# A gated feed-forward stage moved into the attention's block, with its last products in another order

## The reference, cut to what matters

```
x = layernorm(x + attention(x))                  # third norm
gate = silu(x @ dequant(gate_wq, gate_scale).T)  # 512 -> 1376
up   = x @ dequant(up_wq, up_scale).T            # 512 -> 1376
x = layernorm(x + (gate * up) @ dequant(down_wq, down_scale).T)   # 1376 -> 512, last norm
```

## Time and profile before

| | |
|---|---|
| time, median of 3 runs | 2475.66 us (2474.8 to 2475.94) |
| the profiled execution, its own time | 2476.66 us |
| its span, first to last instruction | 2474.6 us |
| PE busy | 2373.2 us, 96% of the span |
| DVE, ACT, POOL busy | 72%, 64%, 51% |
| mean granted clock of PE | 0.984 of full |
| the gated stage, first gate product to the end | 2338.26 us to 2474.6 us |

### The profile page before, as it was taken

One profiled execution on the slowest core, in us unless ns is written; L12 is line 12 of the kernel. 1 busy time (PEld: TensorE's weight loads), 2 busy tenths in 40 slices (PEclk: granted clock), 3 DMA queues, 4 the chain that ended last, 5 costly groups with the idle time before them and its releaser, 6 DMA issues. The chain is left out here.

```text
span 2474.6 us, 48904 instructions
## 1 busy us (share of the span) xinstructions
PE 2373.2 (96%) x15424; PEld 1359.8 (55%) x15624; DVE 1791.4 (72%) x3234; ACT 1591.7 (64%) x3327; POOL 1255.2 (51%) x1002
## 2 busy tenths in 40 slices
PE   6999999999999999999999998789999999999897
PEld 3555555555555555555555555445555555555443
DVE  5677787787777777787777776577777777778522
ACT  7676776776776776776776775365556555656422
POOL 4465555555556556556556569443434343454223
PEclk8999999999999999999999999989999999999899
DMA  7343343343343343343343441320110110100000
GB/s 249 101 132 108 115 130 107 115 131 108 113 133 105 115 133 106 114 134 105 113 134 105 131 146 50 138 89 1 43 44 1 44 44 1 43 18 1 1 0 34
DMA packets 113827, 218.79 MB, mean 88 GB/s; under 512 B 9632, under 2 KB 43040, under 8 KB 111360
## 3 DMA queue, kind: packets, MB, share of 16 engines
q1 hardware_dynamic: 113536, 215.28, 27.0%
HBM read 212.10 MB, written 3.15 MB: 87 GB/s over the span
## 5 line engine op out<-in xcount | busy, mean ns | idle before, releaser
L989 ACT ACTIVATE E<-wq,cst 128x128 f32<-128x128 f32 x1024 | 311.7, 389 | 3.0 <-PEq L298 3.0
L256 DVE SCALAR_TENSOR_TENSOR xc<-bank,taps,xc 128x511 f32<-128x511 f32 (+2 forms) x384 | 284.9, 742 | 35.5 <-ACT xc L243 18.0
L1919 POOL TENSOR_TENSOR qT<-qT,qrot 128x512 f32<-128x512 f32 x64 | 81.2, 1269 | 370.1 <-DVE qrot L1809 370.1
L1282 POOL TENSOR_TENSOR acc<-acc,sq 128x512 f32<-128x512 f32 x112 | 173.1, 1545 | 183.3 <-ACT sq L1001 183.3
L1273 POOL TENSOR_TENSOR xw<-xt,wdec 128x384 f32<-128x384 f32 x128 | 106.4, 831 | 294.1 <-DVE xt L1124 150.7
L1166 DVE SCALAR_TENSOR_TENSOR u<-xc,D,bank 128x512 f32<-128x512 f32 x128 | 95.6, 747 | 205.8 <-PE bank L814 194.2
L1105 DVE TENSOR_TENSOR E<-E,cbm 128x1024 f32<-128x1024 f32 x128 | 242.8, 1897 | 0.8
L59 PE MATMUL bank<-xhi,wx 128*128 128x512 f16 x640 | 242.8, 379 | 0.0
L60 PE MATMUL bank<-xlo,wx 128*128 128x512 f16 x640 | 242.8, 379 | 0.0
L61 PE MATMUL bank<-xhi,wx 128*128 128x512 f16 x640 | 242.6, 379 | 0.0
L1268 POOL TENSOR_TENSOR ecs<-ecs,xcC 128x768 f32<-128x768 f32 x128 | 234.1, 1829 | 0.4 <-POOLq L298 0.4
(11 more groups left out here) (240 smaller groups left out, 6315.0 us busy)
## 6 DMA issues: line engine op xcount, KB each, us to landing
wq<-cs_rows SPq DMA_DIRECT2D x128, 512.0 KB, 4.1
ecs<-ecs_rows SPq DMA_DIRECT2D x128, 384.0 KB, 3.6
wx<-in_w_xbc SPq DMA_DIRECT2D x80, 256.0 KB, 2.7
wz<-in_w_z SPq DMA_DIRECT2D x64, 256.0 KB, 2.7
wo<-in_w_o SPq DMA_DIRECT2D x64, 256.0 KB, 4.0
wq<-in_wq SPq DMA_DIRECT2D x8, 1024.0 KB, 5.8
awo<-in_wo SPq DMA_DIRECT2D x8, 1024.0 KB, 5.0
wkv<-in_wkv SPq DMA_DIRECT2D x8, 512.0 KB, 3.9
```

Source lines behind the costliest of these rows:

```text
L256: self.nc.vector.scalar_tensor_tensor(out=dst[:, d:T], in0=self.k.bank[bank][:, 0:T - d], scalar=self.taps[:, bass.ds(g, 1), b, j, 3 - d:4 ...
L989: ins = nc.scalar.activation(E[t.i % 4][:, h, c], sc.csr[t.i % 2][:, h, c * P:(c + 1) * P], ACT.Relu, scale=-1.0, bias=head(sc.cst, t, c, h))
L1282: nc.gpsimd.tensor_tensor(acc[t.b][:], acc[t.b][:], sq[:], ALU.add).then_inc(acc_done, 1)
```

## The change

It does five things.
- The stage is now the class `Gated`, whose streams are appended to the attention's own, in the same block. The barrier between the two is gone. Its buffers are the attention's: `th` is `qT`, `h` is `qrot`, the halves of the first sequence are `pthi` and `ptlo`, `down` is `probs`.
- `moments` of tiles 6 and 7 move to right behind their `add_output`; gate of n = 0 stands before tile 5's turn; banks are protected by waits on `proj_free` and `ln.lo` in place of the barrier.
- The down weights are cast into `down16`, rows of 512 adjacent 16-bit elements in the tiles of `wq`, all eleven in the last group.
- The second sequence's halves get one buffer for each n (`hi1`, `lo1`), and its down products come after all of its gate and up products, token tile by token tile (22 products each). DVE scales the first sequence's banks after `h` of n = 11, and adds and takes moments of one tile at each of n = 12 to 15; its norm follows at once.
- No loops: all tiles are straight code.

```
@@ attention, PE, DVE, POOL
-                pe.wait_ge(ln.lo, N + 3)
-                ln.turn(pe, 5, k.bank[4], N + 5)
+                ffn.tensor(pe, proj_free, LAST_OUT)
...
+                ffn.scale_tables(dve)
                 for t in range(CH):
                     add_output(1, LAST_OUT + t, (LAST_OUT + t) % 2, t, NG * NB - 1)
-                    if t < 2:
-                        ln.moments(dve, CH + t, N + CH + t)
+                    ln.moments(dve, CH + t, N + CH + t)
                     ln.remainder(dve, 2 + t, k.bank[(4, 2, 3, 4)[t]], N + 2 + t)
+                ffn.vector(dve)
...
+                            if isinstance(g, int) and g == NG - 1:
+                                m = QH * b + h
+                                if m == 0:
+                                    pool.wait_ge(proj_ready, ring(g, 0, 0, 0)[0])
+                                if m == 6:
+                                    pool.wait_ge(proj_ready, ring(g, 1, 1, 0)[0])
+                                convert_down(k, down16, m * IT // 8, (m + 1) * IT // 8)
...
+def convert_down(k, down16, first, end):
+    for i in range(first, end):
+        rows = P if i < IT - 1 else LAST
+        k.nc.gpsimd.tensor_copy(down16[i][0:rows], k.di[0:rows, i]).then_inc(k.d_ok, 1)
@@ Gated.tensor
+        def gate(n):
+            if n < 2:
+                pe.wait_ge(proj_free, last_out + 3 + n)
+            else:
+                pe.wait_ge(self.silu_done, n - 1)
...
+        def up(n):
+            if n < 2:
+                pe.wait_ge(ln.lo, THIRD_NORM + 4 + n)
+            else:
+                pe.wait_ge(self.h_done, n - 1)
...
+        pe.wait_ge(k.gu_ok, 2 * KT)
+        pe.wait_ge(ln.lo, THIRD_NORM + 4)
+        gate(0)
+        ln.turn(pe, 5, k.bank[4], THIRD_NORM + 5)
+        up(0)
+        for t in (6, 7):
+            ln.turn(pe, t, k.bank[t], THIRD_NORM + t)
+        for n in range(1, NB * IT):
+            if n == IT:
+                pe.wait_ge(ln.lo, LAST_NORM)
+            gate(n)
+            up(n)
+            if n == 1:
+                pe.wait_ge(k.d_ok, IT)
+                pe.wait_ge(ln.lo, LAST_NORM)
+            if n <= IT:
+                halves_ready(n - 1)
+                for t in range(CH):
+                    down(n - 1, t)
+        for t in range(CH):
+            pe.wait_ge(self.scaled, t + 1)
+            for n in range(IT, NB * IT):
+                if t == 0:
+                    halves_ready(n)
+                down(n, t)
@@ Gated.vector
+            if n == IT:
+                for m in range(CH):
+                    scale(m)
+            if b and 1 <= i < 1 + CH:
+                m = i - 1
+                add_down(m)
+                dve.wait_ge(self.added, m + 1)
+                ln.moments(dve, m, LAST_NORM + m)
+        for m in range(CH, TT):
+            scale(m)
+            add_down(m)
+            dve.wait_ge(self.added, m + 1)
+            ln.moments(dve, m, LAST_NORM + m)
```

More of the change, by code:

```diff
@@ L1503, in split_first_wo, with attention @@
         self.split(0, 4)
-def attention(k, io, aw):
+def attention(k, io, aw, out):
     nc = k.nc
@@ L1545, in attention @@
         ln, N = k.norms[0], THIRD_NORM
+        down16 = [w[:].bitcast(BF16).rearrange("p k (a n) -> p (k a) n", n=HS)[:, i] for w in wq for i in range(2 * KT)][0:IT]
+        tile16 = ([o[0][:, i] for i in range(QH)] + [x[:] for x in q] + [x[:] for x in kk] + [o[1][:, 0]]
+                  for o, q, kk in ((ohi, qhi, khi), (olo, qlo, klo)))
+        hi1, lo1 = tile16
+        ffn = Gated(k, down16, [x[:] for x in qT], [x[:] for x in qrot], [pthi[:, i * T:(i + 1) * T] for i in range(2)],
+                    [ptlo[:, i * T:(i + 1) * T] for i in range(2)], hi1, lo1,
+                    [x[:, i * T:(i + 1) * T] for x in pr for i in range(2)], tmp)
         def item(g, b, h):
@@ L1612, in _ @@
                 pairs(sp, body)
+                ffn.sync(sp, out)
             @block.tensor
@@ L1800, in _ @@
                     ln.leading(act, t, k.bank[bank], N + t)
+                ffn.scalar(act)
             @block.vector
@@ L1966, in body @@
                                 convert_swiglu(k, pool, item(g, b, h) - item(NG - 2, 0, 0))
+                            if isinstance(g, int) and g == NG - 1:
[5 more added lines that the diff above has]
+                                convert_down(k, down16, m * IT // 8, (m + 1) * IT // 8)
                 pairs(pool, body)
-                for t in range(CH - 1, 6):
+                for t in range(CH - 1, TT):
                     ln.scale_and_shift(pool, t, N + t)
+                ffn.gpsimd(pool)
 INTER = 1376
@@ L2233, in program @@
                 aw.other_buffers(att)
-                attention(k, io, aw)
-            swiglu(k, out)
+                attention(k, io, aw, out)
 def layouts(i):
```

280 lines of the change are left out of this document (106 added, 174 removed).

## The result

The changed kernel takes 2459.86 us (median of 6 runs, 2457.97 to 2461.14), the kernel before in the same session 2475.8 us (6 runs, 2474.8 to 2478.32). The ratio is 0.9933, with a 95% interval of 0.9922 to 0.9944. The forecast was 2461.2, its range 2458.5 to 2464.5.

The account below looks back on a forecast made before the run. PE was taken to bound the gated stage except at the barrier, between the sequences, at n = 21's halves and in the tail. Five terms summed to 14.5 us, 2475.66 to 2461.2 us; 8 in 10 range 2458.5 to 2464.5.

Parts of the forecast that it names:

- 1, head: Start of the gated stage: tile 7's chain to the first silu and first down product comes earlier, -2.7 us.
- 2, packed rows: All 176 down products: adjacent instead of every second 16-bit weight element saves 9.7 ns each, -1.7 us.
- 3, between the sequences: Second sequence's first down product: PE's wait, with DVE's `h` of n = 11 behind the first sequence's sums, goes; -2.9 us.
- 4, halves of n = 21: End of the stage: PE no longer waits for these halves, as 20 other products stand between; -1.2 us.
- 5, tail: After PE's last product: one token tile's chain remains instead of four tiles in a row, 7.43 us for 13.36; -5.9 us.
- the rival of a bound chain: Second sequence's tiles: its chain, not PE, becomes the bound; at 3.9 us a tile 4.5 us lost, 2465.7 us; chance 0.06.
- Half clock in the head: Rival: PE at 1.2 GHz after idle gaps; uncovered after the first down product, 1.6 us lost, 2462.8 us; chance 0.15.
- What was costed at nothing: Casts moved to the attention's last group, scale tables in a DVE gap, straight code for loops: 0 us expected.

Follow-up runs that it names:

- strided: Changed kernel with the down weights cast in place again, so down products read every second 16-bit element; 2461.35 us, ratio 0.9935.
- before_h_first: Kernel before, with the first sequence's four scalings and additions put behind `h` of n = 11 instead of ahead of it; 2471.84 us, ratio 0.9985.
- interleaved: Changed kernel with the second sequence's down products after gate and up of the next tile, as before; 2466.7 us, ratio 0.9959.
- late_moments: Changed kernel, still without the barrier, with moments of tiles 6 and 7 behind tile 5's remainder, as before; 2462.16 us, ratio 0.994.
- scales_first: Changed kernel with the four scalings ahead of `h` of n = 11 again; 2460.35 us, ratio 0.9936.
- barrier: Changed kernel with the barrier back, early moments kept, POOL's scale and shift of tile 7 ahead of the barrier; 2465.24 us, ratio 0.9952.
- before_nmx: Kernel before, with the attention's negated and scaled maxima (`nmx`) computed on ACT instead of DVE; 2474.74 us, ratio 0.9995.
- before: The kernel before the change, unedited, measured in the same session; 2475.8 us.
- before_straight: Kernel before, with the gated stage's loops written out as straight code; 2476.85 us, ratio 1.0002.
- barrier_shift: Changed kernel with the barrier back, early moments kept, POOL's scale and shift of tile 7 behind the barrier; 2461.37 us, ratio 0.9945.
- table: Changed kernel with the silu's table loaded early by a one-column silu behind tile 5's normalising; 2458.6 us, ratio 0.9929.
- best: Changed kernel with early table load, earlier gate of n = 1 and first silu, first down products each waiting for their own bank; 2458.32 us, ratio 0.9923.

## Why the prediction was right, term by term

| term | predicted | measured | by |
|---|---|---|---|
| 1, head | 2.71 | 2.73 | first down product behind the turn, 14.07 to 11.34 |
| 2, packed rows | 1.71 | 1.63 | strided |
| 3, between the sequences | 2.91 | 2.98 | before_h_first |
| 4, halves of n = 21 | 1.24 | 1.28 | interleaved, last product |
| 5, tail | 5.93 | 6.01 | 13.36 to 7.35 |
| sum | 14.49 | 14.63 | stretch as a whole: 14.66 |

The five were measured in different kernels, three by undoing a part of the change and one by doing it alone. That they add up to the whole within 0.1 us is a check and no matter of course.

**Term 1** was right in size and in its chain: the silu comes 7.16 us behind the turn, worked out 7.19. PE's last wait was 1.33 us for 1.6. Of what caused it, the prediction said too little. It followed the chain of tile 7 through the whole change and never asked what each part of the change brings by itself. The parts don't add up: late moments alone bring back 2.65 us of the 2.7 (over ACT's chain), the barrier alone 1.17 (over PE's own work). The two run side by side, so the smaller hides behind the larger. *late_moments* is nearly the kernel before without its barrier, and its first down product is 13.99 us behind the turn for 14.07: almost nothing is gained, though PE's 2.83 us of idle time at the barrier are gone. PE's longest wait there was not the one that set the end.

**Term 2**: the step that two forms of one line led to the earlier trace rows, 9.7 ns, was 9.3 when only the rows changed.

**Term 3**: right, but with two sufficient causes (*before_h_first*, *scales_first*). The prediction's reason, DVE's order, is one of them. No new wait came: PE was busy without a gap through the second sequence's tiles, 3.45 us each, so the rival of a bound chain is out. The prediction had argued so from its 6.9 us of cover.

**Terms 4 and 5**: *interleaved* brings both back, 1.28 and 5.50. The 0.5 us that are missing from 6.01 are POOL's. In the kernel before, the chain that ended last runs through POOL, which computes scale and shift of all eight tiles without a pause, from 2459.60 on. Rows of DVE and POOL for the last tile, kernel before:

```profile
2469.27 0.18 DVE L1384 BATCH_NORM_AGGREGATE n_mv<-n_stats 128x2 f32<-128x6 f32 x1
...
2470.05 0.23 POOL L1402 TENSOR_SCALAR n_rstd<-n_mv 128x1 f32<-128x1 f32 x1
```

POOL takes it up 0.78 us after the aggregate started, for 0.27 in *interleaved* (2460.13 to 2460.40) and in the changed kernel (2453.45 to 2453.72). That is 0.51 us of queue from the first sequence's norm, which has left the tail in *interleaved* too. No run moved that norm alone.

**Half clock in the head** didn't occur in the changed kernel: the gaps were 0.98 and 1.33 us. It did in *barrier*, after 4.47 us, and cost 1.68 us there, since PE was the bound. In *before_nmx* it came at both gaps of that kernel. The second had no cover, as in the case that the rival had priced at 1.6 us, and cost 1.4. The rival was given 0.15; that the changed kernel's two shorter gaps didn't bring it in two traces says little on how often they might.

**What was costed at nothing** held for straight code and for the scale tables, but not for the casts, and there the change gained. The prediction asked only whether moved casts could make `qlo` late (they don't: in the last group PE waits for `qlo` once, 0.82 us, and waited 1.0 before). It didn't ask whom the casts on POOL hold up elsewhere. From the first to the third cast of the up weights, 2241.56 to 2285.78 in *before_nmx*, it takes 44.22 us; in the kernel before 44.74, and 44.24 in the changed one, 44.18 to 44.24 in the others with moved casts. Timelines of DVE and POOL in the changed kernel:

```profile
2245.26 0.52 DVE L1849 TENSOR_SCALAR nmx<-mx 128x4 f32<-128x4 f32 x1
...
2245.14 0.61 POOL L2032 CAST wq<-di 128x512 bf16<-128x512 int32 x1
2245.72 1.16 POOL L1934 TENSOR_TENSOR qlo<-qT,qhi 128x512 f16<-128x512 f32 x1
```

The same two engines in the kernel before:

```profile
2245.59 1.07 DVE L1839 TENSOR_SCALAR nmx<-mx 128x4 f32<-128x4 f32 x1
...
2245.47 1.16 POOL L1923 TENSOR_TENSOR qlo<-qT,qhi 128x512 f16<-128x512 f32 x1
```

An operation on four columns, 0.17 us where POOL is idle, lasts until the POOL operation under way ends: 2246.66 and 2246.63 before, 2245.78 and 2245.75 after. In *strided*, whose cast there lasts 0.75 us, in place, it lasts 0.66 for 0.52. ACT's softmax waits for it. With a short cast in that place instead of the long subtraction, 0.5 us are gained. *before_nmx* takes the operation off DVE and gains the same 0.5 with the old casts, and that shows the cause. The Trainium skill ("SBUF — State Buffer", section Who interferes with whom) has a tensor_scalar in its 2-port mode and GpSimd's accesses exclude each other for a whole instruction; the ends in these rows agree, though no row tells the mode.

**The other 1.2 us ahead of the cut** can't be put down to the change. The kernels differ between the third and the fourth cast of the up weights, where PE is at half clock for some microseconds. POOL's rows, changed kernel:

```profile
2287.74 1.73 POOL L2025 CAST ui<-ui 128x1376 bf16<-128x1376 int32 x1
...
2305.65 1.73 POOL L2025 CAST ui<-ui 128x1376 bf16<-128x1376 int32 x1
```

The kernel before:

```profile
2288.56 1.74 POOL L2005 CAST ui<-ui 128x1376 bf16<-128x1376 int32 x1
...
2307.86 1.73 POOL L2005 CAST ui<-ui 128x1376 bf16<-128x1376 int32 x1
```

That is 17.91 us for 19.30, 1.39 less; the other parts of the last group give 0.15 back. But *before_h_first*, whose attention is that of the kernel before, instruction for instruction, needs 17.72 there. Busy time of PE by window, with the granted clock behind it, first the changed kernel, then the kernel before:

```profile
2298.00:2300.00 2.00, 2.00 (x16) 0.98 0.00 0
```

```profile
2298.00:2300.00 2.00, 2.00 (x10) 0.50 0.00 0
2300.00:2302.00 2.00, 2.00 (x11) 0.57 0.00 0
```

The kernel before is still at half clock where the changed one is back at full. The long passage of 19.2 us or more stands in two of the four traces with the old casts and in none of the ten with the moved ones (17.65 to 18.03). What makes it come stays open, and with it whether the moved casts make it rarer. Turn 4 starts between 2332.16 and 2335.44 in those ten, and between 2330.80 and 2334.90 in the four.

## What to carry to other kernels

Cut the span at an event that both kernels share, and compare what lies behind it: here PE's last product stood 118.19 us behind the cut in both traced executions of the changed kernel, while whole runs spread over 3 us. Where a stage waits at a barrier, follow the chain of the last item as well as the engine that idles: the later of the two sets the end, and removing the other one alone brings next to nothing. And when an operation on POOL is moved or shortened, look for tiny operations on DVE whose length changes with it.

## What the runs showed of the hardware that was not expected

- A `TENSOR_SCALAR` of 128x4 on DVE lasted 0.17 us beside an idle POOL, and up to 1.08 us where it began inside a POOL operation; in the rows shown it ended with that operation within 0.03 us. Where that operation was one of 1.16, 0.75 or 0.61 us, it lasted 1.07, 0.66 and 0.52.
- POOL's cast of 128x512 from int32 to bfloat16 lasts 0.61 us when it writes adjacent elements; two that write every second element in place last 1.44, and two of the new ones 1.17 (changed kernel, 2269.90).
- The same gap had different sequels. PE idles 2.83 us at the barrier in *before*, *before_h_first* and *before_nmx* (2.82 in *before_straight*); behind it products lasted 0.63 us, half clock, in three of the four, and 0.38, full clock, in *before_h_first*. In *barrier_shift* it stayed full after 3.71 us, in *barrier* it fell after 4.47. The length of a gap alone doesn't tell.
- A table load of 1.28 us was had in advance by an activation on one column, 0.20 us, in an idle stretch of ACT (*table*, *best*). The casts and normalisings between it and the silu didn't undo it.
